# Router work moved inside a step of an adaLN attention and expert kernel, and a new order of its last steps

## The chip, the cores and the metric

The kernel runs on one core of a Trainium2 chip. The metric is the device time of one execution in microseconds (us). The kernel before took 1528.84 us, the median of three runs (1527.4 to 1530.59).

## The reference, cut to what matters

One layer on x of 4 batches by 512 rows by 512 columns, float32. Every row is normalised and modulated, goes through causal attention with 32 query heads and 8 key heads of 128 (keys and values from low-rank projections), and then through a router over 64 experts whose chosen weights mix bias rows.

```python
h = _layernorm(x, axis=-1) * (1 + ca) + sa
x = x + ga * _L0_attn_ref(h, ...)
h = _layernorm(x, axis=-1) * (1 + cb) + sb
x = x + gb * _L0_ffn_ref(h, ...)
# _L0_ffn_ref, for T rows:
logits = flat @ router_weight.T + router_bias
topk_w, topk_idx = jax.lax.top_k(softmax(logits), 8)
out = flat * topk_w.sum(-1) + w_dense @ expert_bias
```

## The kernel before, in words

**Steps.** The attention works through 128 query heads (a unit is one key head of one batch, with four query heads; there are 32 units). Each has an index t. The loop runs `step(t)` for t = 0 to 126 on every engine; in it TensorE computes the scores of head t + 1 and work of earlier and later heads. Every product is taken in three passes of a high and a low part (`hi`, `lo`), so each operand is split: ScalarE makes the high part, GpSimd or VectorE the low part by a subtraction.

**One head's way.** TensorE projects q (`q_proj`, L530) into a bank; VectorE multiplies with the rotation tables (L1210 to L1212), GpSimd adds (L1562), ScalarE and GpSimd split (`q_split`, L888, L1567). TensorE computes four row tiles of scores (L579) in the order 3, 2, 1, 0: tile 3 in bank s3, 2 in s2, 1 and 0 in s1. VectorE masks them and takes the row extremes (`mask_and_max`, L1243), ScalarE exponentiates and normalises (L906, L913), VectorE transposes blocks of 32 (L1266), and a DMA through memory finishes the transpose (`PT_raw`, L1851). ScalarE and GpSimd split that into `PT_hi` and `PT_lo` (`split_moved_hi`, L927; `split_moved_lo`, L1574, two halves of 640 columns). Two heads together are multiplied with v (`values_pair`, L612), once for row tiles 2 and 3 (UPPER) and once for 0 and 1 (LOWER), into bank pv; ScalarE and VectorE split the result (OT_hi L937, OT_lo L1274), and `out_pair` (L630) multiplies it with Wo.

**Even and odd steps.** In an even step TensorE runs: scores, `q_proj`, `out_pair` LOWER, router work, `values_pair` UPPER, row transposes. In an odd step: scores, `values_pair` LOWER, `q_proj`, the k or v projection, `out_pair` UPPER, and the transposed weights. The next step's scores follow at once.

**Router work.** From step 92 on, every even step starts one row tile n of 128 rows of the first three batches (12 tiles, `EARLY_TILES`), and its stages lie in later steps. `ffn_gate` (GpSimd, L1596) and `ffn_x1` (VectorE, L1305) form x, statistics follow, ScalarE normalises (`ffn_normal`, L955). TensorE transposes the rows into bank s1 (`ffn_transpose`, L671, for n - 1), ScalarE modulates on the way out (`ffn_modulate`, L970, tile `stage`). `ffn_logits` (L679) writes bank s2 for n - 2; VectorE adds the bias and chooses eight (`ffn_bias`, `ffn_top`); `ffn_weights_T` (L686) and `ffn_mix` (L694, bank s1, for n - 4) mix the expert rows, and VectorE adds the mixture to the output (`finish`, L1394). `fold_experts` (GpSimd, L1623) runs in four steps only. Since router work and scores share s1 and s2, `scores` waits in an odd step for the bias before row tile 2, and for the modulated rows (`h2T_copy`) before row tile 1.

**Order.** Each engine has one queue, written by hand in a program of its own (`tensor_program`, `scalar_program`, `vector_program`, `pool_program`, `sync_program`); an instruction that waits holds all behind it on its engine. Almost all loads and stores are issued by SyncE's queue.

**The end.** Head 127 is transposed by TensorE (L593), the others by DMA. Pair 62 is heads 124 and 125. After the loop come its values and output product, then those of heads 127 and 126 (`values`, `out_last`, L652, L662), and the last four row tiles (12 to 15) go through gate (L1294), router and mixture one after another.

Of the kernel before, what the change touches and what calls it, by code (L numbers as in the profile page):

```python
# [7 lines left out]
F32 = mybir.dt.float32  # L8
# [124 lines left out]
def build(nc, A, out):  # L133
    ctx = ExitStack()
    with ctx:
# [270 lines left out]
        dve_tp, pool_t = sem("dve_tp"), sem("pool_t")  # L406
        pe_s, pe_qp, pe_pv, pe_upper = sem("pe_s"), sem("pe_qp"), sem("pe_pv"), sem("pe_upper")
# [59 lines left out]
        def tensor_program(pe):  # L467
# [128 lines left out]
            def values_pair(p, tiles):  # L596

                t = 2 * p
                pe.wait_ge(pool_t, 2 * (t + 1) + 2)
                if t % GROUP == 0:  # L600
                    pe.wait_ge(dve_v, t // GROUP + 1)
                if pair_done(p, tiles) > 1:
                    pe.wait_ge(dve_o, pair_done(p, tiles) - 1)
                to = bank["pv"][:].rearrange("p (i k) -> p i k", i=2 * SUBS)
                last_key = tiles[-1]
                for kb in range(last_key + 1):
                    first = max(kb, tiles[0])
                    at = KEY_OFFSET[kb] // SUBS + (first - kb) * SUB
                    size = (last_key + 1 - first) * SUB
                    for n, (a, w) in enumerate(passes(v, PT)):  # L610
                        ps = w[:].rearrange("p (i k) -> p i k", i=2 * SUBS)[:, :, at:at + size]
                        mm = pe.matmul(to[:, :, (first - tiles[0]) * SUB:], a[:, kb, :], ps,  # L612
                                       start=(kb == 0 and n == 0), stop=(kb == last_key and n == 2))
                mm.then_inc(pe_pv, 1)
# [22 lines left out]
            def values(t):  # L637

                if moved(t):
                    pe.wait_ge(pool_t, 2 * t + 2)  # L640
                    pe.wait_ge(dve_o, pair_done(PAIRS - 1, LOWER))
                else:
                    pe.wait_ge(dve_e, len(T_PARTS))
# [59 lines left out]
            def step(t):  # L703
# [14 lines left out]
                if h % 2 == 0 and t > 2:  # L718
                    out_pair(t // 2 - 2, LOWER)
# [4 lines left out]
                if h % 2 == 0 and t > 0:  # L724
                    values_pair(t // 2 - 1, UPPER)
                if n is not None:
                    tile_waits((mixed, n - 4), last=EARLY_TILES - 1)
                    ffn_transpose(early(n - 1), "s1")
                if before is not None:
                    pe.wait_ge(dve_s, score_read(t + 1, 0))  # L730
                    ffn_weights_T(early(before - 3), "s1")
# [62 lines left out]
            for j in range(QT):  # L794
                if j == QT - 1:
                    ffn_transpose(EARLY_TILES, "pv")
                for t in (ALL - 1, ALL - 2):
                    out_last(t, j)

# [26 lines left out]
        def scalar_program(act):  # L826
# [165 lines left out]
            def step(t):  # L992
# [9 lines left out]
                if t == ALL - 2:  # L1002
                    split_moved_hi(t - 2)
                if n is not None:
# [5 lines left out]
                if t == ALL - 2:  # L1010
                    split_moved_hi(t - 1)
# [86 lines left out]
            for n in range(len(T_PARTS)):  # L1098
                split_part_hi(n)
            pair_split_hi(PAIRS - 1, LOWER)  # L1100
            split_moved_hi(ALL - 2)
# [22 lines left out]
        def vector_program(dve):  # L1124
# [146 lines left out]

            def pair_split_lo(p, tiles):
# [123 lines left out]
            def step(t):  # L1396
                u, h, n, before = t // GROUP, t % GROUP, ffn_tile(t), ffn_tile(t - 1)
                if h % 2 == 1 and t > 1:
                    pair_split_lo(t // 2 - 1, UPPER)
                mask_and_max(t + 1, 0)  # L1400
                if h % 2 == 0 and t > 2:
# [21 lines left out]
                if n is not None:  # L1423
                    ffn_top(early(n - 3))
                    ffn_bias(early(n - 2), "s2")
                    ffn_minus_max(early(n - 2))
                    finish(early(n - 4), "s1")
                if n is not None:
# [112 lines left out]
        def pool_program(pool):  # L1541
# [117 lines left out]
            def step(t):  # L1659
                u, h, n, before = t // GROUP, t % GROUP, ffn_tile(t), ffn_tile(t - 1)  # L1660
                if h % 2 == 1:
                    if t + 2 < ALL:
                        q_split(t + 2)
                    if before is not None:
                        ffn_gate(early(before))
# [5 lines left out]
                    split_moved_lo(t - 1)  # L1671
# [375 lines left out]
```

## Time and profile before

| | |
|---|---|
| median of three runs | 1528.84 us |
| the profiled execution's own time | 1528.69 us |
| its span, first to last instruction | 1527.4 us |
| PE (TensorE) busy | 1467.5 us, 96% |
| DVE (VectorE) busy | 1147.9 us, 75% |
| ACT (ScalarE) busy | 992.0 us, 65% |
| POOL (GpSimd) busy | 1044.8 us, 68% |
| share of PE in the chain that ended last | 78% |
| mean granted TensorE clock | 0.990 |

Busy is the time in which an engine has an instruction running; several engines are busy at once. The chain that ended last is followed back from the last instruction, at each step to what released it or to the instruction before it on its engine. Idle before an instruction is shown with the instruction that ended it. Ends of matmuls are modelled, so lengths are best read from start to start.

### The profile page before, as it was taken

The numbers are of one execution on the slowest core, as the hardware profiler recorded it, in microseconds if no ns is written. First come the engines' busy times: TensorE is split into PE (matmuls) and PEld (weight loads), VectorE is DVE, ScalarE is ACT, GpSimd is POOL, SyncE is SP. The second block draws the span as 40 slices with busy tenths as digits, with TensorE's granted clock in tenths as the row PEclk, the third lists the DMA queues.
The fourth block names the chain that finished last, engine by engine and source line by source line (L and its number), as shares of the span: only waits on it lengthen the run. The fifth ranks groups of instructions, "written<-read, shape, count | busy, mean of one in ns | idle before, by whom it ended". The sixth has DMA issues, their size and how long they took to land.

```text
span 1527.4 us, 24372 instructions
## 1 busy us (share of the span) xinstructions
PE 1467.5 (96%) x7096; PEld 1223.4 (80%) x7096; DVE 1147.9 (75%) x3443; ACT 992.0 (65%) x2367; POOL 1044.8 (68%) x818
## 2 busy tenths in 40 slices
PE   7878999999999999999999999999999999999986
PEld 4567888888888888888888888888877878788874
DVE  6866777777777777777777777777777888788856
ACT  2256766766667677667677676776666666666663
POOL 1676766766666767667676677665767877777555
PEclk9999999999999999999999999999999999999997
DMA  8636765666666576566576656758786969788760
GB/s 296 220 144 202 218 196 167 210 218 193 199 212 214 180 217 222 158 202 210 179 230 213 198 174 219 218 185 215 229 244 227 284 221 295 240 265 265 236 205 28
DMA packets 214389, 322.55 MB, mean 211 GB/s; under 512 B 41560, under 2 KB 131416, under 8 KB 214256
## 3 DMA queue, kind: packets, MB, share of 16 engines
q1 hardware_dynamic: 213920, 320.87, 66.4%
q8 instruction: 58, 0.95, 0.2%
q14 instruction: 75, 0.61, 0.1%
q10 hardware_dynamic: 336, 0.12, 0.0%
HBM read 179.95 MB, written 140.95 MB: 210 GB/s over the span
## 4 chain that ended last, share of the span: by engine, by line
PE 78%; POOL 7%; DVE 6%; issue 3%; ACT 2%; DMA 2%; SPq 1%; DVEq 0%; POOLq 0%; ACTq 0%
PE bank_s L530 20%; PE bank_o L630 19%; PE bank_pv L612 13%; PE bank_s L579 12%; PE bank_s L553 5%; PE bank_s L541 4%; POOL PT_lo L1574 3%; POOL qT_lo L1567 1%; PE bank_s L507 1%; DMA PT_raw<-blocks 1%; DMA wmod<-in_wmod 1%; PE bank_o L475 1%; ACT stage L970 1%; POOL y L1596 1%; DVE y L1305 1%
## 5 line engine op out<-in xcount | busy, mean ns | idle before, releaser
L1574 POOL TENSOR_TENSOR PT_lo<-PT_raw,PT_hi 128x640 fp32r<-128x640 f32 x252 | 391.1, 1573 | 33.0 <-ACT PT_hi L927 33.0
L913 ACT ACTIVATE probs<-probs,row_inv 128x512 f32<-128x512 f32 (+3 forms) x512 | 258.1, 553 | 210.0 <-DVE row_inv L1249 209.3
L1562 POOL TENSOR_TENSOR rot_c<-rot_c,rot_s 128x512 f32<-128x512 f32 x128 | 168.0, 1312 | 279.9 <-DVE rot_s L1212 279.9
L906 ACT ACTIVATE probs<-probs,row_min 128x512 f32<-128x512 f32 (+3 forms) x512 | 281.3, 552 | 56.3 <-DVE row_min L1243 56.2
L1266 DVE STREAM_TRANSPOSE blocks<-probs 128x384 f32<-128x384 f32 x508 | 213.9, 446 | 18.0 <-ACT probs L913 14.0
L1243 DVE CUSTOM_DVE_ANT_0 probs<-bank_s,mask 128x512 f32<-128x512 f32 (+3 forms) x512 | 226.7, 487 | 0.7 <-issue 0.2
L1567 POOL TENSOR_TENSOR qT_lo<-rot_c,qT_hi 128x512 fp32r<-128x512 f32 x128 | 167.7, 1310 | 63.7 <-ACT qT_hi L888 62.7
L530 PE MATMUL bank_s<-hT_lo,wq_hi 128*128 128x512 f32 x500 | 201.0, 402 | 0.8 <-DVE row_min L1243 0.6
L630 PE MATMUL bank_o<-wo_lo,OT_hi 128*128 128x512 f32 x504 | 196.3, 389 | 2.1 <-DVE OT_lo L1274 2.1
L530 PE MATMUL bank_s<-hT_hi,wq_hi 128*128 128x512 f32 x500 | 196.4, 393 | 0.0
L630 PE MATMUL bank_o<-wo_hi,OT_hi 128*128 128x512 f32 x504 | 196.2, 389 | 0.0
L630 PE MATMUL bank_o<-wo_hi,OT_lo 128*128 128x512 f32 x504 | 196.1, 389 | 0.0
L530 PE MATMUL bank_s<-hT_hi,wq_lo 128*128 128x512 f32 x500 | 195.3, 391 | 0.0
L579 PE MATMUL bank_s<-kT_lo,qT_hi 128*128 128x512 f32 (+3 forms) x512 | 162.7, 318 | 14.2 <-issue 4.6
L927 ACT ACTIVATE PT_hi<-PT_raw 128x640 fp32r<-128x640 f32 x252 | 170.8, 727 | 5.3 <-DMA PT_raw<-blocks 5.0
L1210 DVE TENSOR_TENSOR rot_c<-bank_s,cos_t 128x512 f32<-128x512 f32 x125 | 86.2, 690 | 106.5 <-PE bank_s L530 106.5
L579 PE MATMUL bank_s<-kT_hi,qT_hi 128*128 128x512 f32 (+3 forms) x512 | 165.6, 323 | 0.0
L579 PE MATMUL bank_s<-kT_hi,qT_lo 128*128 128x512 f32 (+3 forms) x512 | 165.1, 322 | 0.0
L1274 DVE TENSOR_TENSOR OT_lo<-bank_pv,OT_hi 128x512 fp32r<-128x512 f32 x126 | 86.7, 688 | 104.3 <-ACT OT_hi L937 104.3
L612 PE MATMUL bank_pv<-PT_lo,v_hi 128*128 128x512 f32 x378 | 140.0, 370 | 13.5 <-DVE OT_lo L1274 6.8
L612 PE MATMUL bank_pv<-PT_hi,v_hi 128*128 128x512 f32 x378 | 135.3, 358 | 0.0
L612 PE MATMUL bank_pv<-PT_hi,v_lo 128*128 128x512 f32 x378 | 135.1, 357 | 0.0
(252 smaller groups left out, 3224.8 us busy)
## 6 DMA issues: line engine op xcount, KB each, us to landing
blocks<-blocks SPq DMA_DIRECT2D x127, 640.0 KB, 3.0
PT_raw<-blocks SPq DMA_DIRECT2D x504, 160.0 KB, 3.6
stage<-in_wq SPq DMA_DIRECT2D x32, 256.0 KB, 4.8
vblocks<-kv_raw SPq DMA_DIRECT2D x32, 256.0 KB, 5.0
kv_raw<-vblocks SPq DMA_DIRECT2D x128, 64.0 KB, 2.0
stage<-in_wo SPq DMA_DIRECT2D x32, 256.0 KB, 4.9
split_wq<-wq_hi SPq DMA_DIRECT2D x32, 256.0 KB, 4.6
split_wq<-wq_lo SPq DMA_DIRECT2D x32, 256.0 KB, 5.5
```

The lines of the kernel that those rows point to most:

```text
L530: mm = pe.matmul(q_bank(t)[:], w[:, h, c, :], x[:, b * CH + c, :], start=(c == 0 and n == 0), stop=(c == CH - 1 and n == 2))
L579: mm = pe.matmul(score_bank[qt], q[:, qt * P:(qt + 1) * P], k[:, 0:(qt + 1) * P], start=(n == 0), stop=(n == 2))
L612: mm = pe.matmul(to[:, :, (first - tiles[0]) * SUB:], a[:, kb, :], ps, start=(kb == 0 and n == 0), stop=(kb == last_key and n == 2))
L630: mm = pe.matmul(bank[f"o{j}"][:], o[:, o_at:o_at + P], w[:, h, :], start=(h == 0 and n == 0), stop=(h == GROUP - 1 and n == 2))
L906: ins = act.activation(row(t, qt), row(t, qt), ACT.Exp, bias=row_min[m][:, qt:qt + 1], scale=-1.0, accum_out=row_sum[m][:, qt:qt + 1])
L913: ins = act.activation(row(t, qt), row(t, qt), ACT.Copy, scale=row_inv[t % 2][:, qt:qt + 1])
L927: act.activation(parts_of(t)[0][:, at], raw_of(t)[:, at], ACT.Copy).then_inc(act_t, 1)
L1243: dve.tensor_tensor_reduce(row(t, qt), score_bank[qt], mask[:, SEQ - (qt + 1) * P:], -SCALE, -LOWEST, ALU.add, ALU.min, row_min[m][:, qt:q ...
L1266: ins = dve.transpose(blocks_v[:, qt:qt + 3 * whole_keys - 2:3], keys[:, 0:whole_keys])
L1562: pool.tensor_tensor(rot_c[:], rot_c[:], rot_s[:], ALU.add).then_inc(pool_a, 1)
L1567: pool.tensor_tensor(lo[:], rot_c[:], hi[:].bitcast(F32), ALU.subtract).then_inc(pool_q, 1)
L1574: pool.tensor_tensor(lo[:, at], raw_of(t)[:, at], hi[:, at].bitcast(F32), ALU.subtract).then_inc(pool_t, 1)
```

## The change

TensorE: in an even step mixture and logits come right after `q_proj`, then `out_pair` LOWER, the row transposes, and `values_pair` UPPER last. VectorE: in an even step `finish` stands ahead of `ffn_top`, bias and `keep`. GpSimd: in an odd step `ffn_gate` is first. In step 126 (`ALL - 2`) VectorE takes OT_lo of pair 61 LOWER before its masks and the low part of head 124 between the two mask halves (new function, new semaphore `dve_t`), and ScalarE takes PT_hi of head 125 ahead of the exponentials. After the loop ScalarE splits head 126 before the last OT_hi, and TensorE transposes tile 12 after all of `out_last`.

```diff
             def values_pair(p, tiles):
 
                 t = 2 * p
-                pe.wait_ge(pool_t, 2 * (t + 1) + 2)
+                if p < PAIRS - 1:
+                    pe.wait_ge(pool_t, 2 * (t + 1) + 2)
+                else:
+                    pe.wait_ge(dve_t, 2)
+                    pe.wait_ge(pool_t, 2 * (t + 1))
...
                 if moved(t):
-                    pe.wait_ge(pool_t, 2 * t + 2)
+                    pe.wait_ge(pool_t, 2 * t)
...
                     out_pair(t // 2 - 1, UPPER)
-                if h % 2 == 0 and t > 2:
-                    out_pair(t // 2 - 2, LOWER)
                 if n is not None:
                     pe.wait_ge(dve_s, score_read(t + 1, 0))
                     ffn_mix(early(n - 4), "s1")
                     ffn_logits(early(n - 2), "s2")
-                if h % 2 == 0 and t > 0:
-                    values_pair(t // 2 - 1, UPPER)
+                if h % 2 == 0 and t > 2:
+                    out_pair(t // 2 - 2, LOWER)
                 if n is not None:
                     tile_waits((mixed, n - 4), last=EARLY_TILES - 1)
                     ffn_transpose(early(n - 1), "s1")
+                if h % 2 == 0 and t > 0:
+                    values_pair(t // 2 - 1, UPPER)
...
             for j in range(QT):
-                if j == QT - 1:
-                    ffn_transpose(EARLY_TILES, "pv")
                 for t in (ALL - 1, ALL - 2):
                     out_last(t, j)
+            ffn_transpose(EARLY_TILES, "pv")
...
                 if t == ALL - 2:
                     split_moved_hi(t - 2)
+                    split_moved_hi(t - 1)
...
                 exponentials(t + 1, 1)
-                if t == ALL - 2:
-                    split_moved_hi(t - 1)
...
+            split_moved_hi(ALL - 2)
             pair_split_hi(PAIRS - 1, LOWER)
-            split_moved_hi(ALL - 2)
...
+            def split_moved_lo(t):
+                for half in range(2):
+                    at = slice(half * CAUSAL // 2, (half + 1) * CAUSAL // 2)
+                    dve.wait_ge(act_t, 2 * t + half + 1)
+                    hi, lo = parts_of(t)
+                    dve.tensor_tensor(lo[:, at], raw_of(t)[:, at], hi[:, at].bitcast(F32), ALU.subtract).then_inc(dve_t, 1)
...
+                if t == ALL - 2:
+                    pair_split_lo(t // 2 - 2, LOWER)
                 mask_and_max(t + 1, 0)
-                if h % 2 == 0 and t > 2:
+                if t == ALL - 2:
+                    split_moved_lo(t - 2)
+                elif h % 2 == 0 and t > 2:
                     pair_split_lo(t // 2 - 2, LOWER)
...
                 if n is not None:
+                    finish(early(n - 4), "s1")
                     ffn_top(early(n - 3))
                     ffn_bias(early(n - 2), "s2")
                     ffn_minus_max(early(n - 2))
-                    finish(early(n - 4), "s1")
-                if n is not None:
                     keep(early(n - 3))
...
                 if h % 2 == 1:
+                    if before is not None:
+                        ffn_gate(early(before))
                     if t + 2 < ALL:
                         q_split(t + 2)
                     if before is not None:
-                        ffn_gate(early(before))
                         ffn_split_weights(early(before - 3))
...
-                    split_moved_lo(t - 1)
+                    if t + 1 < ALL - 2:
+                        split_moved_lo(t - 1)
```

## Rows read from the trace of the kernel before

**Rows 1.** Stages: length, PE, PEld, DVE, ACT, POOL busy (x); PEclk, DMA share, GB/s.

```profile
700.00:1000.00 300.00, 300.00 (x1463) 255.04 (x1462) 222.99 (x694) 209.38 (x497) 206.14 (x151) 1.00 0.64 202
1200.00:1300.00 100.00, 95.38 (x475) 79.02 (x473) 84.12 (x259) 65.65 (x165) 77.79 (x72) 1.00 0.83 263
1477.00:1479.00 2.00, 2.00 (x6) 1.62 (x7) 0.00 (x0) 0.00 (x0) 1.92 (x2) 0.64 1.02 276
```

**Rows 2.** Timeline of TensorE: first score matmul of ten steps (start us, us, what).

```profile
700.10 0.39 PE L579 MATMUL bank_s<-kT_lo,qT_hi 128*128 128x512 f32 x1
...
711.27 0.39 PE L579 MATMUL bank_s<-kT_lo,qT_hi 128*128 128x512 f32 x1
...
721.05 0.39 PE L579 MATMUL bank_s<-kT_lo,qT_hi 128*128 128x512 f32 x1
...
1090.34 0.39 PE L579 MATMUL bank_s<-kT_lo,qT_hi 128*128 128x512 f32 x1
...
1263.31 0.47 PE L579 MATMUL bank_s<-kT_lo,qT_hi 128*128 128x512 f32 x1
...
1274.93 0.49 PE L579 MATMUL bank_s<-kT_lo,qT_hi 128*128 128x512 f32 x1
...
1287.41 0.47 PE L579 MATMUL bank_s<-kT_lo,qT_hi 128*128 128x512 f32 x1
...
1385.57 0.47 PE L579 MATMUL bank_s<-kT_lo,qT_hi 128*128 128x512 f32 x1
...
1396.83 0.39 PE L579 MATMUL bank_s<-kT_lo,qT_hi 128*128 128x512 f32 x1
...
1408.38 0.47 PE L579 MATMUL bank_s<-kT_lo,qT_hi 128*128 128x512 f32 x1
```

**Rows 3.** Groups on TensorE, 1090 to 1465 us: busy, mean | idle before, releasers.

```profile
L579 PE MATMUL bank_s<-kT_lo,qT_hi 128*128 128x512 f32 (+3 forms) x128 | 43.4, 339 | 5.2 <-ACT stage L970 3.2 <-DVE kv_rot L1221 1.2 <-issue 0.5
...
L612 PE MATMUL bank_pv<-PT_lo,v_hi 128*128 128x512 f32 x96 | 36.5, 380 | 8.4 <-DVE OT_lo L1274 6.4 <-POOL PT_lo L1574 1.8
```

**Rows 4.** Timeline, 1272 to 1279 us, three engines: [idle before <-releaser].

```profile
1272.62 0.69 DVE L1394 TENSOR_TENSOR h<-bank_s,h 128x512 f32<-128x512 f32 x1
...
1275.21 1.50 ACT L970 ACTIVATE stage<-bank_s,modT_rows 128x128 f32<-128x128 f32 x4 [3.82 <-PE bank_s L671]
...
1276.77 0.39 PE L579 MATMUL bank_s<-kT_lo,qT_hi 128*128 128x256 f32 x1 [0.36 <-ACT stage L970]
...
1277.24 0.69 DVE L1274 TENSOR_TENSOR OT_lo<-bank_pv,OT_hi 128x512 fp32r<-128x512 f32 x1 [1.61 <-ACT OT_hi L937]
...
1278.08 0.47 PE L612 MATMUL bank_pv<-PT_lo,v_hi 128*128 128x512 f32 x1 [0.40 <-DVE OT_lo L1274]
```

**Rows 5.** Timeline of GpSimd at 709 us and VectorE at 1280 us.

```profile
709.86 3.10 POOL L1574 TENSOR_TENSOR PT_lo<-PT_raw,PT_hi 128x640 fp32r<-128x640 f32 x2 [0.37 <-ACT PT_hi L927]
...
1280.37 0.70 DVE L1305 TENSOR_TENSOR y<-y,stage 128x512 f32<-128x512 f32 x1 [0.77 <-POOL y L1596]
...
1281.97 1.07 DVE L1232 TENSOR_TENSOR v_lo<-kv_raw,v_hi 128x512 fp32r<-128x512 f32 x1
```

**Rows 6.** Timeline of step 126: four engines.

```profile
1469.48 0.69 DVE L1243 CUSTOM_DVE_ANT_0 probs<-bank_s,mask 128x512 f32<-128x512 f32 x1
...
1469.55 1.36 ACT L927 ACTIVATE PT_hi<-PT_raw 128x640 fp32r<-128x640 f32 x2 [0.80 <-DMA PT_raw<-blocks]
...
1471.31 0.50 PE L630 MATMUL bank_o<-wo_lo,OT_hi 128*128 128x512 f32 x1 [2.10 <-DVE OT_lo L1274]
...
1473.81 3.04 POOL L1574 TENSOR_TENSOR PT_lo<-PT_raw,PT_hi 128x640 fp32r<-128x640 f32 x2 [0.35 <-ACT PT_hi L927]
...
1476.90 0.50 PE L612 MATMUL bank_pv<-PT_lo,v_hi 128*128 128x512 f32 x1 [2.55 <-POOL PT_lo L1574]
```

**Rows 7.** Timeline of VectorE in the last 25 us.

```profile
1503.58 0.69 DVE L1294 TENSOR_TENSOR x_end<-bank_o,gate 128x512 f32<-128x512 f32 x1 [0.81 <-PE bank_o L662]
...
1507.64 0.16 DVE L1337 RECIPROCAL small<-small 128x1 f32<-128x1 f32 x1 [1.31 <-ACT logit L978]
```

More of the change, by code:

```diff
@@ L406, in build @@
         dve_tp, pool_t = sem("dve_tp"), sem("pool_t")
+        dve_t = sem("dve_t")
         pe_s, pe_qp, pe_pv, pe_upper = sem("pe_s"), sem("pe_qp"), sem("pe_pv"), sem("pe_upper")
```

## The prediction, made before the change was run

> **What bounds the kernel now.** I read the busy shares by stage first, then the step lengths, then TensorE's waits, then who releases them. A change is worth 0.2% (3.1 us) or more before a measurement of this kernel tells it from none.
>
> Through the attention-only stage TensorE is busy all the time at full clock; between 1200 and 1300 it is 95.4 of 100 us [rows 1]. So the question is only what TensorE loses late. A step is counted from one first score matmul to the next. Without router work an odd step takes 711.27 - 700.10 = 11.17 us and an even one 721.05 - 711.27 = 9.78 us [rows 2]. The plain even step has 21504 moving columns, so 0.455 ns each: scores 1.75, q_proj 2.79, out_pair LOWER 2.79, values_pair UPPER 2.45. Router work adds the mixture, 1024 columns or 0.47; with mixture and logits a step takes 1396.83 - 1385.57 = 11.26, so the logits cost 1.01; with all three and no wait 1274.93 - 1263.31 = 11.62, so the row transposes cost 0.36. An odd step late in this stretch, after the transposes have ended, takes 1408.38 - 1396.83 = 11.55.
>
> From 1090.34 to 1385.57 lie 24 steps, 295.23 us. Floor: odd, 2 x 11.17 + 10 x 11.55 = 137.84 (the transposed weights run in ten); even, one with transposes only (10.14), two with logits too (2 x 11.15), nine with all (9 x 11.62), together 137.02. That is 274.86, so **20.37 us** are lost here. The idle time named for TensorE is only 13.6 [rows 3]; the rest is restart after a wait, since the ends of matmuls are modelled.
>
> One step shows it [rows 4]: the row transposes are last in the even step, ScalarE's four modulated copies run 1275.21 to 1276.71, and the scores of row tile 1, which share the bank, wait until 1276.77. ScalarE takes OT_hi only after the copies, VectorE's OT_lo starts at 1277.24, and values_pair LOWER waits again, to 1278.08. The odd step becomes 1287.41 - 1274.93 = 12.48, 0.93 over its floor. The delay runs on: masking starts only after OT_lo, x1 waits 0.77 for GpSimd's gate, which stands behind q_split and so behind ScalarE [rows 5], rope comes late, then GpSimd's PT_lo and the k rotation, which explain the waits of even steps [rows 3].
>
> **The change, part by part.**
>
> *TensorE's order in an even step.* No work is added. Mixture and logits now start 4.54 into the step, out_pair at 6.02, transposes at 8.81, values_pair at 9.17. The copies on ScalarE (1.50) fit under values_pair UPPER and end near 10.8, against 11.62 for the step's end; h2T_copy and OT_hi are then ready when asked for. Both waits of the odd step go.
>
> *VectorE's sum first.* The transposes need s1 free, so they now wait for the sum in the middle of the step. The sum starts 1272.62 - 1263.31 = 9.31 into the step now [rows 4]. Moved ahead of the top-8 work and the bias it follows the rope: q_proj ends at 4.54, three products of about 0.69, a reciprocal, so from about 7.0 to 7.7. TensorE asks at 8.81: 1.1 us of cover. Behind the sum, top-8 and bias end where they did, since the logits no longer come last; the next reader of s2 is in the odd step, 2 us later. The mixture asks for row tile 0's mask at 4.54; OT_lo and the masks are done near 3.5. Cost nothing, cover 1 us; without it each us late is a us per step.
>
> *Gate first on GpSimd.* It needs sums two or more steps old, so it can run before the odd step's q_split. x1 loses its wait of 0.77 [rows 5]. q_split comes 1.29 later behind it than it could, but its reader is scores of the next step, over 6 us away. SP's loads of x wait on x1, so they only move earlier; no DMA is added.
>
> *What is left of the 20.37.* The odd waits and their restarts go in full. GpSimd is the next late engine: from the rope on it has rope, PT_lo (3.10 in two halves), q_split, the small ones, in four pairs the fold, PT_lo again, and in every other even step the k rotation and k split before the next scores. In an unstalled odd step the first PT_lo starts 709.86 - 700.10 = 9.76 into it [rows 5]. Behind it come 3.10, q_split and fold at about 1.3 each (PT_lo's 1.55 for 640 columns, scaled to 512), small ones that I take at 1.2, and 3.10 again: 19.8, which is 8.2 into the even step, before values_pair at 9.17. The k rotation, ScalarE's kT_hi and the k split (1.3, 0.7, 1.3 by the same scale) then end near 11.6, or 12.4 if VectorE is 0.8 late, against 11.62. Two fold steps have both: 0 to 1.6 us. VectorE operations with two SBUF inputs also stretch: v_lo took 1.07 where its like take 0.69 [rows 5], and rope behind it slips; 0 to 2 us more. I take 18.0 of 20.37; bounds 12.0 (the odd waits alone, about 1.0 in each of 12 pairs) and 20.5.
>
> *Last two steps.* out_pair(61, LOWER) now waits until 1471.31 and values_pair(62, UPPER) until 1476.90 [rows 6]. With OT_lo before the masks it starts at 1469.48 instead of after masks of 0.69 and 0.55: out_pair starts 1.1 earlier. What holds the second wait is GpSimd, which splits head 124 and then 125 (3.04). VectorE takes 124 (two halves, 0.69 x 640/512 = 0.86 each), and ScalarE does PT_hi of 125 right after 124's, at 1470.91 or when its load lands; that load was issued up to 2 us behind 124's, which landed at 1469.5, so about 1471.5. GpSimd's 3.04 then runs from 1472.3 to 1475.4: 1.5 us earlier. Behind the VectorE wait stand the masks of half 1, and behind ScalarE's moved 1.36 the last head's exponentials; its rows are normalised near 1477.3 instead of 1476.2, and TensorE asks for them only after values_pair, near 1478. Cover 0.7. TensorE's clock was granted at 0.64 from 1477 to 1479 [rows 1], that is partly 1.2 GHz, after those two idle stretches. If the shorter idle keeps 2.4 GHz, another 1.6 us goes; if VectorE's split is held, the gain shrinks to 0. I take **1.5**, bounds 0 and 3.1.
>
> The two-input splits of head 124 are where a rule bears. The Trainium skill, SBUF — State Buffer, section "Who interferes with whom", says that a VectorE instruction with two SBUF inputs and a GpSimd instruction that reads SBUF lock each other out for a whole instruction. By that rule the second half could stand behind one 1.52 us half of GpSimd's, which would take the last head past its cover and 0.8 off the 1.5; v_lo's 1.07 agrees that such an operation is held.
>
> *The end.* PT_late_hi moves before the last OT_hi on ScalarE, into time when ScalarE waits for TensorE: nothing. Row transposes of tile 12 after the last out_last: VectorE's wait of 0.81 for the fourth bank goes, but the chain then waits 1.31 for the exponentials, which stand on ScalarE behind GpSimd's small operations [rows 7]. Cover 1.31 over 0.81: nothing, bounds 0 and 0.8.
>
> **Sum.** 18.0 + 1.5 = 19.5. The profiled execution took 1528.69, the median is 1528.84, so the two stand 0.15 apart; 1528.84 - 19.5 = **1509.3 us**.
>
> **Rivals.**
> - *The even waits stay.* The k split and PT_lo on GpSimd remain the limit in most pairs: 12.0 + 0 to 1.5, so 1515.5 to 1517. For it: GpSimd is at 78% in this stage [rows 1], and it holds the fold. Against: the even steps with 11.62 wait for nothing although their odd step was late. Chance 0.12.
> - *Loads become the limit.* DMA share is 0.83 here against 0.64 [rows 1], and a shorter step asks for the same bytes sooner. PT_hi would wait: at 1469.55 it waited 0.80 for its load [rows 6]. At 0.8 in each of 12 pairs 9.6 us come back: about 1519. Against: from 700 to 1000 the same sequence ran at full speed, and idle of that kind is rare. Chance 0.05.
> - *The meeting in the middle costs more than it gives (slower).* In nine steps TensorE's transposes wait for VectorE's sum, with all of values_pair behind them. If the sum kept its present end, 10.0, the loss would be 1.2 x 9 = 10.7 us, and the total is still faster. It decides when the sum ends later than 8.81 + 19.5/9 = 11.0; at 11.2 it gives 1531 us. For it: everything on VectorE is queued in order, so a late rope makes a late sum. Against: the rope waits for q_proj alone. Chance 0.03.
> - *It only moves the wait.* The odd step loses its first wait, but OT_lo stays late because VectorE ends its blocks late, and values_pair LOWER waits as before; gain under 3 us, 1526 to 1531. Against: VectorE waited 1.61 for OT_hi before that OT_lo [rows 4], so it was free. Chance 0.03.
>
> **The numbers.** Forecast 0.77, the rivals 0.12, 0.05, 0.03 and 0.03. Faster: 0.77 + 0.12 + 0.05 = 0.94; same 0.03; slower 0.03. Range: low end 20.5 + 3.1 = 23.6 of gain, 1505.2; high end takes in the first rival and stops short of the loads, 1518.
>
> **What would show it.** Right: odd steps with router work at about 11.5 instead of 12.48; no TensorE wait for ScalarE's stage or for OT_lo in them; x1 with no wait on GpSimd; even steps at 11.6; out_pair(61, LOWER) about 1.1 and values_pair(62, UPPER) about 1.5 us earlier, counted from the scores before them; the last 31 us unchanged. Wrong: a TensorE wait for VectorE's sum before the row transposes, waits for kT_lo at the start of most even-odd turns, or PT_hi waiting for loads in every pair.

## The result, and the profile of the changed kernel

| | before | changed |
|---|---|---|
| median, same chip | 1528.12 us (1526.04 to 1530.59, 4 runs) | 1508.13 us (1506.83 to 1510.86, 4 runs) |
| profiled execution, its span | 1528.69, 1527.4 us | 1506.83, 1505.5 us |
| 24 steps from index 95 to 119 | 295.23 us | 276.95 us |
| PE share of the chain that ended last | 78% | 88% |

The ratio is 0.9871 (95% interval 0.985 to 0.9891): 20.0 us or 1.3% faster, where 19.5 was forecast. The page's parts 1 and 4 of the changed kernel, then its windows with the columns of [rows 1]:

```profile
PE 1463.4 (97%) x7096; PEld 1225.0 (81%) x7096; DVE 1148.6 (76%) x3445; ACT 993.8 (66%) x2367; POOL 1042.3 (69%) x816
...
PE 88%; DVE 4%; POOL 3%; issue 2%; ACT 1%; DMA 1%; SPq 0%; DVEq 0%; ACTq 0%; POOLq 0%
```

```profile
700.00:1000.00 300.00, 300.00 (x1462) 255.00 (x1461) 223.84 (x695) 208.98 (x497) 205.46 (x150) 1.00 0.64 202
1200.00:1300.00 100.00, 99.52 (x504) 84.30 (x503) 87.99 (x274) 71.79 (x179) 84.63 (x76) 1.00 0.88 282
1457.00:1459.00 2.00, 2.00 (x8) 1.58 (x7) 0.08 (x1) 0.51 (x2) 1.92 (x2) 0.65 0.95 236
```

The attention-only stage is as it was. In the router stage TensorE has gone from 95.38 to 99.52 us in 100, and the same busy time lies closer together on GpSimd (77.79 to 84.63) and in the DMA share (0.83 to 0.88). The third row is the stretch behind the last idle of TensorE, [rows 1]'s third: the granted clock is still at 0.65 there.

The two spans differ by 21.9 us (the profiled execution of the changed kernel is 1.3 under its median). Counted from one first score matmul to the next: 1.5 lie ahead of index 95 (the traces of the kernels below, whose work there is all but the same, lie from 0.9 above to 1.7 below the kernel before, so it is scatter), **18.3 in the 24 steps**, 0.1 from index 119 to 126, 1.7 from there to the first gate of the end, 0.25 behind that. The timeline of TensorE, the first score matmuls of heads 95, 109, 110, 111 and 119 (the step that opens with the scores of head 109 is an even one, t = 108):

```profile
1088.81 0.39 PE L581 MATMUL bank_s<-kT_lo,qT_hi 128*128 128x512 f32 x1
...
1249.73 0.47 PE L581 MATMUL bank_s<-kT_lo,qT_hi 128*128 128x512 f32 x1
...
1261.48 0.39 PE L581 MATMUL bank_s<-kT_lo,qT_hi 128*128 128x512 f32 x1
...
1272.69 0.47 PE L581 MATMUL bank_s<-kT_lo,qT_hi 128*128 128x512 f32 x1
...
1365.76 0.47 PE L581 MATMUL bank_s<-kT_lo,qT_hi 128*128 128x512 f32 x1
```

The even step takes 1261.48 - 1249.73 = 11.75 and the odd one 1272.69 - 1261.48 = 11.21; the same pair took 11.62 and 12.48 before [rows 2]. The groups of [rows 3] over 1088 to 1441 us show why: TensorE waits for neither ScalarE's stage nor, but for 0.8 us, VectorE's OT_lo.

```profile
L581 PE MATMUL bank_s<-kT_lo,qT_hi 128*128 128x512 f32 (+1 forms) x124 | 39.5, 319 | 0.9 <-issue 0.9
...
L618 PE MATMUL bank_pv<-PT_lo,v_hi 128*128 128x512 f32 x93 | 35.3, 380 | 1.0 <-DVE OT_lo L1285 0.8
```

The timeline of that pair of steps on four engines answers to [rows 4, 5]:

```profile
1256.88 0.67 DVE L1405 TENSOR_TENSOR h<-bank_s,h 128x512 f32<-128x512 f32 x1
...
1258.37 1.31 POOL L1610 TENSOR_TENSOR y<-y,gate 128x512 f32<-128x512 f32 x1
...
1258.59 0.60 PE L677 MATMUL bank_s<-ident,normal 128*128 128x128 f32 x4
...
1259.23 1.51 ACT L975 ACTIVATE stage<-bank_s,modT_rows 128x128 f32<-128x128 f32 x4 [1.43 <-PE bank_s L677]
...
1262.31 0.69 DVE L1285 TENSOR_TENSOR OT_lo<-bank_pv,OT_hi 128x512 fp32r<-128x512 f32 x1 [0.43 <-ACT OT_hi L942]
...
1264.59 0.72 DVE L1316 TENSOR_TENSOR y<-y,stage 128x512 f32<-128x512 f32 x1
...
1264.71 1.75 POOL L1654 TENSOR_TENSOR h<-normal,scale 128x512 f32<-128x512 f32 x1
```

The sum ends 7.8 us into the even step; the transposes start at 8.86, 1.0 behind it, and wait for nothing (in three of the nine full even steps both come 0.16 to 0.24 later). ScalarE's four copies end at 11.0, 0.7 before the next scores. GpSimd runs the gate in the even step's end, so x1, 3.1 into the odd step, has no wait where it had 0.77. The last row is taken up at the end: that operation usually takes GpSimd 1.29.

### The profile page after: what moved, and what is told of

It reads as the page before. It is cut to its first block, busy times and chain, and to the rows that moved or that the text cites. A ratio compares the mean times of both kernels' runs of the same rounds, so it can differ in the third digit from the quotient of the medians.

```text
span 1505.5 us, 24375 instructions
## 1 busy us (share of the span) xinstructions
PE 1463.4 (97%) x7096; PEld 1225.0 (81%) x7096; DVE 1148.6 (76%) x3445; ACT 993.8 (66%) x2367; POOL 1042.3 (69%) x816
## 4 chain that ended last, share of the span: by engine, by line
PE 88%; DVE 4%; POOL 3%; issue 2%; ACT 1%; DMA 1%; SPq 0%; DVEq 0%; ACTq 0%; POOLq 0%
PE bank_s L532 23%; PE bank_o L636 22%; PE bank_s L581 15%; PE bank_pv L618 14%; PE bank_s L555 6%; PE bank_s L543 5%; POOL PT_lo L1588 1%; PE bank_s L509 1%; DMA wmod<-in_wmod 1%; PE bank_o L477 1%; DVE y L1183 1%; PE bank_s L685 1%; POOL hT_lo L1566 0%; POOL qT_lo L1581 0%; DVE h_raw L1195 0%
```

## The experiments

Each kernel is named by what it does; a step has the index of the head whose scores open it, t + 1, so the even steps with router work are indices 95, 97 and so on. Lengths are of profiled executions, times are medians beside the kernel before on the same chip, and "the changed kernel" has the stretch of 276.95 us above.

**TensorE's order alone** (on the kernel before):

```diff
-                if h % 2 == 0 and t > 2:
-                    out_pair(t // 2 - 2, LOWER)
                 if n is not None:
...
-                if h % 2 == 0 and t > 0:
-                    values_pair(t // 2 - 1, UPPER)
+                if h % 2 == 0 and t > 2:
+                    out_pair(t // 2 - 2, LOWER)
...
                     ffn_transpose(early(n - 1), "s1")
+                if h % 2 == 0 and t > 0:
+                    values_pair(t // 2 - 1, UPPER)
```

> The kernel before with TensorE's new order in the even steps alone; VectorE's sum stays behind top-8 and bias, the gate stays behind q_split, the end stays old. Theory (the odd waits come from the late row transposes, and the sum must be early to allow them): TensorE is ready for the transposes 8.8 us into an even step, the sum ends at 10.0, so nine even steps wait about 1.2 us for it, 10 to 11 us in all, while the odd waits go. Stretch of 24 steps near 286 us (295.2 before, 277.0 after the whole change); time 8 to 11 us below before, a TensorE wait for the sum in each full even step. Rival (the sum has no part in it; the order alone brings all): stretch 277 to 279, time 17 to 18 us below before.

Measured: 1524.07 us against 1528.48, ratio 0.9969 (0.9957 to 0.9981), the stretch 289.16. The odd steps from index 102 on take 11.20 to 11.21 (96 and 100 take 11.30 and 11.86, in the changed kernel 11.31 and 11.82). The nine full even steps take 12.27 to 13.70 instead of 11.75 to 11.98. A group and one instance of it on TensorE:

```profile
L671 PE MATMUL bank_s<-ident,normal 128*128 128x128 f32 x48 | 7.7, 283 | 8.5 <-DVE h L1394 8.5
```

```profile
1171.00 0.66 PE L671 MATMUL bank_s<-ident,normal 128*128 128x128 f32 x4 [0.97 <-DVE h L1394]
```

So both odd waits go with TensorE's order alone, and without the sum first the meeting in the middle takes most of the gain back. The loss was larger than expected: 8.5 us of named wait, and 2.3 more behind the stretch.

**Sum and gate first, TensorE's order as before**, and **the gate alone**:

```diff
                 if n is not None:
+                    finish(early(n - 4), "s1")
                     ffn_top(early(n - 3))
                     ffn_bias(early(n - 2), "s2")
                     ffn_minus_max(early(n - 2))
-                    finish(early(n - 4), "s1")
...
                 if h % 2 == 1:
+                    if before is not None:
+                        ffn_gate(early(before))
                     if t + 2 < ALL:
                         q_split(t + 2)
                     if before is not None:
-                        ffn_gate(early(before))
```

(the second kernel has the lower half of it alone)

> The kernel before with the sum first on VectorE and the gate first on GpSimd, TensorE's order old, the end old. Theory: the sum finds its mixture late (TensorE computes it after out_pair, 8 us into the step), so VectorE waits for it with top-8 and bias behind; the odd waits for the modulated rows and OT_lo stay at about 1.0 us a pair. Gate first takes 0.8 off VectorE's odd step and with it some of the 8 us of even waits. Time 0 to 4 us below before. Rival (VectorE's and GpSimd's order bring the gain): 10 us or more below before.

> The kernel before with only the gate first on GpSimd. Theory (the gate alone gives what sum and gate gave together, since the sum was not waited for): even steps with router work come down as they did there, odd ones stay near 12.5; stretch 290 to 291.5 us, time 3 to 4.5 us below before. Rival (the sum's place gave it): stretch 294 or more.

Measured: 1524.52 us (ratio 0.9973, 0.9961 to 0.9985) and 1523.73 (0.9969, 0.9957 to 0.9981); stretches 290.49 and 290.66. Odd steps stay near 12.5 in both. What goes is waits of even steps: index 97 falls from 12.39 to 11.12 to 11.16, 99 from 13.49 to 12.3, and 103, 105 and 115 to 11.62 to 11.65. With the old order of TensorE, then, the gate is worth 4.6 us and the sum nothing; moving the sum as well even costs 1.8 between indices 119 and 126 (77.86 against 76.05 with the gate alone).

**All of the change but the gate's move:**

```diff
                 if h % 2 == 1:
-                    if before is not None:
-                        ffn_gate(early(before))
                     if t + 2 < ALL:
                         q_split(t + 2)
                     if before is not None:
+                        ffn_gate(early(before))
```

> The changed kernel with the gate back behind q_split on GpSimd. Theory: with OT_hi and q_split early, the gate is only some 0.6 us late for VectorE, which has about as much slack before the rope; stretch of 24 steps 277 to 279 us, time 0 to 2 us above the changed kernel. Rival (the gate was what held VectorE and so GpSimd's later split): odd and even steps each lose about 0.7, stretch 285 or more, time 8 us or more above it.

Measured: 1512.65 us, ratio 0.9891 (0.9876 to 0.9906), the stretch 281.55. Odd steps are as in the changed kernel or up to 0.2 shorter, but even steps 95, 97, 99, 105 and 111 take 11.74, 12.23, 13.38, 12.28 and 12.57, against 10.68, 11.19, 12.10, 11.75 and 11.94 there. The timeline of VectorE and a group on TensorE:

```profile
1200.99 0.69 DVE L1316 TENSOR_TENSOR y<-y,stage 128x512 f32<-128x512 f32 x1 [1.10 <-POOL y L1610]
```

```profile
L618 PE MATMUL bank_pv<-PT_lo,v_hi 128*128 128x512 f32 x96 | 36.3, 378 | 1.7 <-POOL PT_lo L1588 0.9 <-DVE OT_lo L1285 0.8
```

The gate is worth 281.55 - 276.95 = 4.6 us here too. x1 starts 3.97 to 5.05 into the odd step instead of 3.11 to 3.93, behind waits of 0.56 to 1.10 for the gate, and what stands behind it on VectorE, the rope of q among it, is late for the GpSimd splits that the even step needs. At index 98 the rope starts at 7.37 instead of 6.12 and the next PT_lo at 11.19 instead of 9.94. At index 96 it is more than the wait: x1 also runs beside GpSimd's product there and takes 1.76 instead of 0.79, so the rope is 2.03 late. The same 4.6 with and without TensorE's new order: this part adds to the others, whichever comes first.

**Dose: the sum behind the top-8 work.** The changed kernel with one line moved:

```diff
                 if n is not None:
-                    finish(early(n - 4), "s1")
                     ffn_top(early(n - 3))
+                    finish(early(n - 4), "s1")
```

> The changed kernel with VectorE's sum one place later, behind the top-8 work and still ahead of the bias. Theory (TensorE's row transposes wait for the sum once it ends later than 8.8 us into an even step): the sum now ends at 7.8; top-8 takes 1.5 to 2.4 us, so it ends at 9.3 to 10.2 and nine full steps wait 0.5 to 1.4 us; stretch of 24 steps 282 to 288 us (277.0 with the whole change), time 5 to 11 us above the changed kernel, less than the 12 us or so that the sum's old place cost with the new order of TensorE. Rival (the meeting has slack, since values_pair can absorb it): within 2 us of the changed kernel.

Measured: 1517.44 us against 1527.85, ratio 0.9923 (0.9902 to 0.9945); the stretch 282.82, 5.9 longer. The timeline of VectorE and TensorE in one step, and the group:

```profile
1215.90 0.69 DVE L1405 TENSOR_TENSOR h<-bank_s,h 128x512 f32<-128x512 f32 x1
...
1216.64 0.66 PE L677 MATMUL bank_s<-ident,normal 128*128 128x128 f32 x4 [0.62 <-DVE h L1405]
```

```profile
L677 PE MATMUL bank_s<-ident,normal 128*128 128x128 f32 x48 | 7.7, 283 | 5.7 <-DVE h L1405 5.7
```

The transposes start 0.05 to 0.06 behind the sum's end, 9.44 to 10.13 into the step instead of 8.86 to 9.10, and the nine even steps with all the work take 12.38 to 13.07 instead of 11.75 to 11.98: in the mean they start 0.75 later and the step is 0.78 longer. Odd steps from index 102 on stay at 11.2. So the cover of 1.0 us is real, and what the sum is late beyond it is added to each such step. Another 2.1 us go in the even steps of indices 119 and 121, behind the stretch, where no transposes stand but TensorE still waits for the sum.

**The fold moved on GpSimd**, out of the odd step's end to between k rotation and k split, where GpSimd waits for ScalarE:

```diff
-                    if t + 1 - FFN_FROM in EXPERT_STEPS:
-                        fold_experts(EXPERT_STEPS.index(t + 1 - FFN_FROM))
                 if h % 2 == 0:
...
                         k_rope(u + 1)
+                    if t - FFN_FROM in EXPERT_STEPS:
+                        fold_experts(EXPERT_STEPS.index(t - FFN_FROM))
+                    if h == 2 and u + 1 < UNITS:
                         k_split(u + 1)
```

> The changed kernel with the fold of the experts moved on GpSimd from the end of the odd step into the even step, behind PT_lo and the k rotation, where GpSimd waits for ScalarE's kT_hi. Theory (in the fold steps GpSimd's k split is what the next scores wait for): kT_lo in the two fold steps that hold a k split ends 1.2 us earlier, at most 11 us into the step, the waits of 0.6 at the following scores go, the even steps of 12.10 and 11.95 come down to 11.75 to 11.9 and the odd ones of 11.8 to 11.2 to 11.4; 1.0 to 1.5 us off the stretch of 277.0. Rival (VectorE, not GpSimd, sets these steps): step lengths as before, nothing gained.

Measured: 1505.96 us against 1527.85, ratio 0.9855 (0.9837 to 0.9872); the stretch 275.63, 1.3 shorter. The changed kernel's steps with both fold and k split (99 and 100: 12.10 and 11.82) become 11.84 and 11.28; of 111 and 112 (11.94 and 11.82) the second becomes 11.27 and the first stays. The four traces with the changed kernel's loop spread over 276.95 to 277.66, so 1.3 is the least of it; the kernel further down that moves the fold too has 275.24. The timeline of GpSimd at the first:

```profile
1143.66 1.31 POOL L1637 TENSOR_TENSOR experts_in<-experts_in,gate 128x512 f32<-128x512 f32 x1
...
1144.90 1.76 POOL L1597 TENSOR_TENSOR kT_lo<-kv_raw,kT_hi 128x512 fp32r<-128x512 f32 x1
```

The fold now fills a gap of 0.74 in which GpSimd waited for ScalarE's kT_hi. The k split behind it takes 1.76, where it took 1.28 in the changed kernel, which gives part of it back.

**The new order of the end alone** (the loop as before). The diff is that of the change without its parts for even and odd steps of the router stage.

> The kernel before with only the new orders of step 126 and the end. Theory: out_pair(61, LOWER) 1.1 to 1.3 us earlier after the start of the last-but-one scores, values_pair(62, UPPER) 0.9 to 1.5 earlier, first gate of the last tiles 1.7 earlier; time 1.5 to 2 us below before. Rival (the last 30 us give it back, since the clock is granted lower there): first gate 1.7 earlier but time within 0.5 us of before.

Measured: 1527.31 us against 1528.48, ratio 0.9989 (0.998 to 0.9999). Counted from the scores of head 126: out_pair(61, LOWER) at +8.60 (before +9.84), values_pair(62, UPPER) at +14.68 (+15.43), the first gate at +33.45 (+34.42); the stretch behind the first gate 29.23 (29.44). The time is 1.2 us below the kernel before (0.1 to 3.1 by the interval), less than the 1.5 to 2 expected.

**GpSimd keeps head 124.** The changed kernel with `split_moved_lo(t - 2)` on VectorE taken out again, its waits with it:

```diff
                 if t == ALL - 2:
-                    split_moved_lo(t - 2)
...
-                    if t + 1 < ALL - 2:
-                        split_moved_lo(t - 1)
+                    split_moved_lo(t - 1)
```

> The changed kernel with GpSimd splitting both heads 124 and 125 in step 126; OT_lo first and PT_hi of 125 early stay. Theory (GpSimd starts 124 as soon as its first PT_hi is there, 0.8 us after 1449.5, and needs 3.05 us a head): it ends 125 some 6.9 us after, near 1456.4, so values_pair(62, UPPER) starts 14.9 to 15.0 us after the scores of head 126's step begin against 14.57 with VectorE's share; 0.4 us, not seen in the time. Rival (VectorE's share is worth its full 1.5 us or more): start at 16 or later.

**The changed kernel once more**, with the exact edit of the change:

> The changed kernel again, unaltered, beside the run before it. Theory: 18 to 21 us below before; stretch of 24 steps within 0.3 of 276.95; the 117 us ahead of the stretch within 1 us of the kernel before, so the 1.5 us that the first profile of the changed kernel was ahead there was scatter. Rival (it gains ahead of the stretch too): again 1.5 us ahead there.

Measured: 1508.85 us (ratio 0.9875, 0.9858 to 0.9892) and 1509.13 (0.9874, 0.9859 to 0.9889). The first has values_pair(62, UPPER) at +15.01, against +14.57 in the changed kernel and +14.68 in the one with the end alone: VectorE's share is worth 0.2 to 0.4 us there (the repeat has +14.76), not the larger part of 1.5. Yet its first gate is at +32.26, earlier than in the changed kernel (+32.72) and its repeat (+34.12). The windows show what differs, first of the kernel in which GpSimd keeps the head, then of the repeat (columns as in [rows 1]):

```profile
1458.00:1460.00 2.00, 1.42 (x6) 1.20 (x7) 1.19 (x3) 1.62 (x4) 1.79 (x2) 1.00 1.00 238
1460.00:1462.00 2.00, 2.00 (x16) 1.82 (x15) 0.03 (x1) 0.66 (x2) 1.92 (x3) 1.00 0.83 258
```

```profile
1456.00:1458.00 2.00, 0.65 (x2) 0.58 (x3) 1.18 (x4) 2.00 (x8) 1.37 (x2) 0.62 0.95 261
1458.00:1460.00 2.00, 2.00 (x6) 1.57 (x5) 0.33 (x1) 0.76 (x3) 1.92 (x2) 0.50 1.04 295
1460.00:1462.00 2.00, 2.00 (x8) 1.66 (x7) 0.00 (x0) 0.00 (x0) 1.92 (x3) 0.50 0.11 32
```

In the repeat the granted clock falls to 0.50 (1.2 GHz) toward the end of an idle stretch of TensorE of 3.15 us, 0.9 before it takes up work, and it then does 8 matmuls in 2 us; in the other kernel it stays at 1.00 (2.4 GHz) behind one of 3.40 and does 16. The first gates differ by 1.9 us, more than was planned for these steps. The repeat's stretch of 24 steps is 277.09, 0.14 from the changed kernel's; the kernel in which GpSimd keeps the head has 277.66. The scatter ahead of index 95 shows as well: it is 0.6 below the kernel before in the repeat, 1.7 below in the kernel with the gate alone and 0.9 above in the one with the sum behind the top-8 work.

**Tile 12's transposes before the last bank**, as in the kernel before:

```diff
             for j in range(QT):
+                if j == QT - 1:
+                    ffn_transpose(EARLY_TILES, "pv")
                 for t in (ALL - 1, ALL - 2):
                     out_last(t, j)
-            ffn_transpose(EARLY_TILES, "pv")
```

> The changed kernel with the row transposes of tile 12 back in front of out_last of the fourth bank. Theory (the chain of the last 30 us does not pass through the fourth bank): from the first gate to the last sum 29.2 us as now, within 0.3; the fourth gate comes 0.8 later without consequence. Rival (moving them lost TensorE's clock in the last 25 us, 0.53 granted against up to 1.0 from 1504 to 1510 before): with the old order the clock is back at 1.0 for some us and the tail is 0.5 us or more shorter.

Measured: 1510.28 us against 1527.85, ratio 0.988 (0.9862 to 0.9899). From the first gate to the last sum it takes 28.99 us, against 29.19 in the changed kernel: the fourth gate comes 7.19 behind the first instead of 6.79, and nothing that ends last asks for it. The move is worth nothing measurable, either way. The rival falls too: with the old order the granted clock is 0.50 from 1484 us to the end, as in the changed kernel (0.52 over its last 25 us), where the kernel before had 0.93 from 1504 to 1510.

**The fold moved, and the exponentials of tile 12 ahead of the modulation of tile 13** on ScalarE:

```diff
-            ffn_modulate(b, "s3")
             ffn_exp(a)
+            ffn_modulate(b, "s3")
```

> The changed kernel with the fold moved as in the run before, and in the last tiles the exponentials of tile 12 ahead of the modulated copies of tile 13 on ScalarE. Theory (VectorE waits 2.1 us for those exponentials, which stand behind copies that they do not need, and VectorE's queue sets the end from there): the exponentials start near 9.9 us after the first gate instead of 11.1, VectorE's top-8 work of tile 12 1.2 us earlier, first gate to last sum 28 to 28.5 us against 29.2; time 2 to 3 us below the changed kernel, 1.3 of it the fold. Rival (tile 13's copies, 0.4 us later, carry the end): tail 29.2 to 29.6, time 1 to 1.5 us below the changed kernel.

Measured: 1506.51 us against 1528.89, ratio 0.9861 (0.9844 to 0.9877). The exponentials come 9.75 after the first gate instead of 11.1, and VectorE's choice at 10.2 instead of 11.6. Only 0.3 of it is left at the end (28.92; 28 to 28.5 was expected). A VectorE row of each of the two tiles:

```profile
1485.01 1.20 DVE L1380 TENSOR_TENSOR weight<-rest,weight 128x64 fp32r<-128x64 f32 x1
...
1491.52 1.76 DVE L1397 SCALAR_TENSOR_TENSOR h<-h,small,y 128x512 f32<-128x512 f32 x1
```

The first is no loss, it took 1.22 in the changed kernel. The second took 0.74 there; beside one of GpSimd's operations it takes 1.76, and of the 1.3 us by which VectorE was still ahead before it 0.3 are left behind it.

On the same chip this kernel's four runs (1505.64 to 1508.05) lie below the repeat's four (1508.31 to 1509.71), 2.6 us between the medians. It is the fastest beside the one with the fold alone; the ratios' intervals overlap with the changed kernel's.

## Why the prediction was right, point by point

**Where the 20.37 us went.** The stretch gave 18.28 against 18.0 taken. The runs allow it to be laid out in the order in which parts were added. Of the close agreement (20.0 against 19.5) part is luck, as the terms below show: the 18.0 rests on two errors of about 2 us against each other, and in the profiled execution the last steps had a favourable clock.

| | stretch, us | gives |
|---|---|---|
| before | 295.23 | |
| TensorE's order | 289.16 | 6.1 |
| with the sum first | 281.55 | 7.6 |
| with the gate first | 276.95 | 4.6 |

The first two need each other: the sum alone gives nothing (290.49 with it, 290.66 without, both with the gate), the order alone leaves 8.5 us of new waits. The last row adds up alone and together. (The middle row has the new end too, which lies behind the stretch.)

**TensorE's order**: right. Mechanism, places and durations came within 0.2 us: transposes at 8.86 (8.81), copies' end at 11.0 (10.8). One size was off in each direction. The floor of the full even step is 11.75, not 11.62: the same matmuls in the new order take 0.13 longer, which the step "no work is added" left out; nine such steps cost 1.2 us (where it lies is told at the end). The floor of the odd step is 11.21 and not the 11.55 read from a late odd step of the kernel before, which still held a wait: its values_pair LOWER starts 0.3 later behind the scores than in the new kernel. Ten of those are 3.4 us the other way. With these two the floor of the stretch is 274.86 + 1.2 - 3.4 = 272.7, so the kernel before stood 22.6 us above it, not 20.37, and 4.3 are left, not 2.4. That the floor was 2.2 too high and what stays 1.9 too low nearly cancels in the forecast; that is luck and not insight.

**The sum first**: right, with 7.8 for its end (7.7) and a cover of 1.0 (1.1). The slower rival named this meeting, and its price per us is what the dose shows. Its point of decision, 11.0, was borne out roughly: with the sum's end at 9.6 in the mean, 0.8 past TensorE's 8.8, the medians lose 9.6 of the 20.0 us and the traces 8.0 (5.9 in the stretch, 2.1 behind it). By these slopes the rest would be gone at 10.5 to 10.8, an estimate.

**The gate first**: this is the step that was mis-sized. The prediction counted x1's 0.77 and gave the move no term of its own, and my expectation of the kernel without it was 0 to 2 us. It is 4.6, all of it in even steps (95 to 99, 105 and 111 above all): x1 stands ahead of the rope on VectorE, so its wait delays the rope of q, PT_lo and the k split by as much or, where it also meets GpSimd's product, by up to 2.0. The prediction did say that the delay runs on in this way; it did not put a price on it. The forecast held since the gain was taken as a whole, from floors.

**What stays**: of those 4.3 us, 2.4 lie in the two pairs of steps with fold and k split (99 and 100, 111 and 112), as named, for which 0 to 1.6 had been set. Of the rest 0.5 lie in index 95 and about 0.2 each in six more steps (102, 103, 107, 108, 114, 115). Moving the fold takes off 1.3 us net. The timeline of GpSimd and TensorE in the changed kernel, at the turn from index 99 to 100:

```profile
1143.88 1.28 POOL L1597 TENSOR_TENSOR kT_lo<-kv_raw,kT_hi 128x512 fp32r<-128x512 f32 x1 [0.74 <-ACT kT_hi L899]
...
1145.27 0.47 PE L581 MATMUL bank_s<-kT_lo,qT_hi 128*128 128x512 f32 x1 [0.60 <-issue]
```

The k split ends at 1145.16, 0.11 before the scores that read it.

**The last steps**: 1.5 was taken, 1.7 came in the profiled executions and 1.0 in the kernel with the end alone. The thirteen traces narrow this down. In ten of them the granted clock is at 0.50 for 3 to 4 us that begin 14.6 to 16.1 us after the scores of head 126: there the first gate comes at +34.14 to +34.42 with the old end (three kernels) and at +32.72 to +33.49 with the new one (seven, the middle one +33.40). So the new end is worth about 0.85 us, the 1.7 holds some luck with the clock, and the 1.6 that the prediction allowed for a clock that stays up did not come: the changed kernel has 0.65 from 1457 to 1459, the kernel before 0.64 in its like. What the edits themselves give is in the timeline of four engines, the counterpart of [rows 6]:

```profile
1449.44 0.65 DVE L1285 TENSOR_TENSOR OT_lo<-bank_pv,OT_hi 128x512 fp32r<-128x512 f32 x1
...
1449.53 1.37 ACT L932 ACTIVATE PT_hi<-PT_raw 128x640 fp32r<-128x640 f32 x2 [0.69 <-DMA PT_raw<-blocks]
...
1450.15 0.50 PE L636 MATMUL bank_o<-wo_lo,OT_hi 128*128 128x512 f32 x1 [0.85 <-DVE OT_lo L1285]
...
1451.12 1.56 DVE L1281 TENSOR_TENSOR PT_lo<-PT_raw,PT_hi 128x640 fp32r<-128x640 f32 x2
...
1452.16 1.37 ACT L932 ACTIVATE PT_hi<-PT_raw 128x640 fp32r<-128x640 f32 x2 [1.26 <-DMA PT_raw<-blocks]
...
1452.98 3.04 POOL L1588 TENSOR_TENSOR PT_lo<-PT_raw,PT_hi 128x640 fp32r<-128x640 f32 x2 [8.74 <-ACT PT_hi L932]
...
1456.12 0.47 PE L618 MATMUL bank_pv<-PT_lo,v_hi 128*128 128x512 f32 x1 [2.94 <-issue]
```

out_pair is 1.24 us earlier (1.1 forecast): right. values_pair is 0.86 earlier (1.5): ScalarE waits 1.26 for the load of head 125, so PT_hi starts at 1452.16. From the scores of head 126 at 1441.55 that is 10.6, where the prediction had taken the load 0.6 earlier. So that step failed by 0.6, the load's landing, which its own text had as a guess of up to 2 us.

**The rule on SBUF.** VectorE's two halves of head 124 took 1.56 together, 0.78 each, undisturbed, since GpSimd was idle until 1452.98. The rule of the Trainium skill (SBUF — State Buffer, "Who interferes with whom") had no case to bite on in this place. It did elsewhere, as the part on the hardware shows.

**The end**: nothing was forecast and 0.25 us came, within the bounds of 0 and 0.8. The wait for the fourth bank has gone and that for the exponentials has grown, as the timeline of VectorE shows beside [rows 7]:

```profile
1485.85 0.16 DVE L1348 RECIPROCAL small<-small 128x1 f32<-128x1 f32 x1 [2.06 <-ACT logit L983]
```

2.06 here is the 0.81 and 1.31 of before in one wait, 0.06 short of their sum.

**The rivals.** That even waits stay did not happen, but it would have in part without the gate's move. Loads did not become the limit in the stretch: no group of TensorE's waits there names them; one place at the end does.

## What to carry to other kernels

When a consumer of a shared buffer stands last in a step, the next step pays for the whole chain behind it. Moving it to the middle pays in full only if the producer that it meets there is moved as well (6.1 us of the stretch alone, 13.7 with both): price the meeting in time of arrival, since up to the cover it costs nothing and beyond it each us costs one. A short wait on an engine that is not the bound is priced by what stands behind it in that engine's queue: 0.6 to 1.1 us before each x1 were worth 4.6 us over 12 pairs of steps. And a floor read from a late step of the old kernel can still hold a wait that the profile doesn't name (11.55 read, 11.21 real).

## What the runs showed of the hardware that was not expected

**TensorE's clock does not follow from the last idle stretch alone.** Windows of the repeat and of the kernel in which GpSimd keeps head 124:

```profile
1456.50:1463.20 6.70, 5.84 (x18) 5.01 (x19) 1.71 (x4) 2.99 (x9) 5.84 (x5) 0.50 0.57 157
```

```profile
1443.50:1484.00 40.50, 32.86 (x171) 27.11 (x171) 22.23 (x59) 20.88 (x47) 24.96 (x24) 1.00 0.44 132
```

Of the thirteen traces eleven have the clock at 0.50 for 3 to 4 us in these steps, the repeat for nearly 7, and the one with the longest idle there (3.40 us) not at all. In the kernel with sum and gate alone the fall comes sooner, 1.2 us after TensorE has taken up work behind an idle of 2.11; the other kernels with the old end keep 1.00 there, behind 2.10. What decides it was not found. The first gate lies at +32.26 without the fall and at +34.12 with the longest, so an edit of a few tenths in these steps can only be read from places ahead of the fall, or from many traces.

**VectorE and GpSimd hold each other up both ways, and the length can be worked out.** GpSimd's product of 128x512 took 1.75 beside VectorE's x1, and kT_lo 1.76, against 1.28 to 1.31 alone; VectorE's product of 64 columns took 1.20 against 0.23, and its h of 128x512 1.76 against 0.74. In each of these pairs the one that starts second is longer by what is left of the first, less 0.13 to 0.19 us: x1 has 0.60 left when GpSimd's product starts, which takes 0.46 longer; GpSimd's operation has 1.13 left when VectorE's product of 64 columns starts, which takes 0.97 longer. By the rule of the Trainium skill (SBUF — State Buffer, "Who interferes with whom"), one instruction shuts the other engine out for its whole length, and these rows agree with it.

**The order of matmuls has a price of its own.** The even step with all its work takes 11.75 in the new order and 11.62 in the old, both without a named wait. The timelines place it, from start to start: in all nine such steps of the changed kernel out_pair takes 2.85 to 2.86 behind the logits, where it took 2.72 behind q_proj, while in a step that loses nothing else (index 109) each of the other groups agrees to 0.02. Its first matmul is followed by the next after 0.31 instead of 0.23 (rows from 1255.74 in the changed kernel and from 1268.06 before). Why it is so, no run shows.

```profile
1255.74 0.48 PE L636 MATMUL bank_o<-wo_lo,OT_hi 128*128 128x512 f32 x1
1256.05 0.39 PE L636 MATMUL bank_o<-wo_hi,OT_lo 128*128 128x512 f32 x1
```

```profile
1268.06 0.39 PE L630 MATMUL bank_o<-wo_lo,OT_hi 128*128 128x512 f32 x1
1268.29 0.39 PE L630 MATMUL bank_o<-wo_hi,OT_lo 128*128 128x512 f32 x1
```
